# A mixture-of-experts layer on one core: packed expert numbers, a longer loop, and redrawn head, lists and last stores

## What is computed

```python
def cond(x, w, W_base, b_base, As, Bs):              # w: 64 x 8, one row for each sequence of 64 tokens
    out = einsum('btc,oc->bto', x, W_base) + b_base
    h = einsum('btc,erc->bter', x, As)
    return out + einsum('bter,eor,be->bto', h, Bs, w) * 2.0
def ffn(x1):
    scores = softmax(x1 @ gate_w.T)                   # 8 scores for each token
    topk_w, topk_i = top_k(scores, 2)
    topk_w = topk_w / (topk_w.sum(-1) + 1e-20) * 2.5
    y = sum over the two: topk_w * ((silu(x1 @ w_gate[e]) * (x1 @ w_up[e])) @ w_down[e])
    return y + (silu(x1 @ sw_gate) * (x1 @ sw_up)) @ sw_down
return x + ffn(cond(x, cond_8, ...))
```

## Time and profile before

| | |
|---|---|
| median of three runs | 510.59 us (508.84, 510.59, 510.64) |
| the profiled execution | 506.99 us, its span 505.3 us |
| TensorE, matmuls | busy 490.5 us, 97% |
| TensorE, weight loads | busy 448.2 us, 89% |
| VectorE | busy 355.4 us, 70% |
| ScalarE | busy 261.1 us, 52% |
| GpSimd | busy 249.9 us, 49% |
| instruction fetches | q8: 17 of 0.28 MB in all; q14: 21 of 0.17 MB |
| granted TensorE clock, mean | 0.999 |

### The profile page before, as it was taken

The page is one execution under the profiler, slowest core; times in us unless marked ns, Lnnn a source line. Parts: engine busy times, 40 slices in busy tenths (PEclk is TensorE's granted clock), DMA queues, the critical chain, the costliest instruction groups (busy, mean ns, idle before and its releaser), DMA issues.

```text
span 505.3 us, 10018 instructions
## 1 busy us (share of the span) xinstructions
PE 490.5 (97%) x3071; PEld 448.2 (89%) x3072; DVE 355.4 (70%) x765; ACT 261.1 (52%) x525; POOL 249.9 (49%) x367
## 2 busy tenths in 40 slices
PE   8999999999999999989999999999999899999996
PEld 7998988888888889988889999999998899888886
DVE  3666778898987556766676677676675666479896
ACT  3567785556663445565455555545554444444322
POOL 2042246655551454666967767677667674211100
PEclk9999999999999999999999999999999999999999
DMA  8387569156222234534344444444444442599942
GB/s 225 130 281 224 169 186 310 57 179 201 45 83 43 84 93 126 119 103 125 104 114 116 114 116 123 123 117 117 112 114 116 115 105 68 145 370 322 384 140 83
DMA packets 104938, 74.54 MB, mean 148 GB/s; under 512 B 61946, under 2 KB 99844, under 8 KB 104900
## 3 DMA queue, kind: packets, MB, share of 16 engines
q1 hardware_dynamic: 95780, 55.21, 37.1%
q0 software_dynamic: 6816, 18.62, 12.5%
q10 hardware_dynamic: 2304, 0.26, 0.5%
HBM read 40.25 MB, written 20.32 MB: 120 GB/s over the span
## 4 chain that ended last, share of the span: by engine, by line
PE 75%; DVE 15%; ACT 5%; issue 4%; DMA 1%; another core or an unknown queue 0%; DVEq 0%; ACTq 0%
PE bank L274 17%; PE bank L276 17%; PE bank L275 17%; PE bank L790 9%; PE bank L762 5%; PE bank L792 5%; DVE bank L1222 2%; ACT gt_h L952 1%; DVE acc L1333 1%; DVE xt_l L1034 1%; ACT x_half L872 1%; DVE x L1058 1%; DVE pos L1081 1%; DMA xin<-in_x_dram 1%; PE bank L576 1%
## 5 line engine op out<-in xcount | busy, mean ns | idle before, releaser
L274 PE MATMUL bank<-w_all,rt_h 128*128 x284 | 97.6, 344 | 0.0
L276 PE MATMUL bank<-w_all,rt_l 128*128 x284 | 91.6, 323 | 0.0
L275 PE MATMUL bank<-w_all,rt_h 128*128 x284 | 91.5, 322 | 0.0
L790 PE MATMUL bank<-w_all,gt_h 128*128 (+1 forms) x213 | 78.0, 396 | 0.2 <-issue 0.2
L551 POOL DMA_INDIRECT y_rows<-y_sb,dst_i x71 | 72.5, 1021 | 11.2 <-POOL spare L465 10.4
L544 POOL DMA_INDIRECT rows<-x_halves,tok_i x71 | 69.5, 978 | 12.5 <-issue 2.2
L952 ACT CAST gt_h<-bank 128x512 fp32r<-128x512 f32 (+1 forms) x48 | 28.1, 586 | 88.7 <-DVE bank L1222 79.8
L274 PE MATMUL bank<-xs_h,sg_h 128*128 128x512 f32 x176 | 70.6, 401 | 0.3 <-DVE gt_h L1233 0.3
L275 PE MATMUL bank<-xs_l,sg_h 128*128 128x512 f32 x176 | 68.9, 391 | 0.0
L276 PE MATMUL bank<-xs_h,sg_l 128*128 128x512 f32 x176 | 68.7, 390 | 0.0
L1295 DVE TENSOR_TENSOR g<-bank,act 128x352 f32<-128x352 f32 x71 | 37.2, 524 | 41.7 <-issue 24.5
(11 more groups left out here) (180 smaller groups left out, 1155.6 us busy)
## 6 DMA issues: line engine op xcount, KB each, us to landing
pick<-y_rows SPq DMA_DIRECT2D x16, 512.0 KB, 7.8
xin<-in_x_dram SPq DMA_DIRECT2D x8, 512.0 KB, 4.8
x_halves<-x_half SPq DMA_DIRECT2D x8, 512.0 KB, 3.3
w_own<-in_L_ffn_w_gate_dram SPq DMA_DIRECT2D x8, 352.0 KB, 4.5
w_own<-in_L_ffn_w_up_dram SPq DMA_DIRECT2D x8, 352.0 KB, 4.7
y_sb<-in_x_dram SPq DMA_DIRECT2D x5, 512.0 KB, 3.5
base_rows<-y_sb SPq DMA_DIRECT2D x5, 512.0 KB, 2.8
acc<-base_rows SPq DMA_DIRECT2D x5, 512.0 KB, 7.1
```

Of the source, the lines that this page charges most:

```text
L274: pe.matmul(o, lh, rh, start=start, stop=False, skip_group_check=skip)
L275: pe.matmul(o, lh, rl, start=False, stop=False, skip_group_check=skip)
L276: return pe.matmul(o, ll, rh, start=False, stop=stop, skip_group_check=skip)
L790: pe.matmul(YE[par][:, 0:2 * D].rearrange("p (h d) -> p h d", h=2), gt_h[par][0:n, cols], both, start=(c == 0), stop=False, skip_group_che ...
```

## The change

- *Head.* On SP: W_base first, then x in two loads of 256 rows with a semaphore each (`s_x_two`, `s_xin[0]`), then cond, then bias. g_raw and b_row go to ACT's queue, ahead of lora_b. TensorE turns W_base, g_raw and b_row before x, x in halves, with the folds between. ScalarE and VectorE take the halves of W_base (`base_high`, `base_low`) around those of x.
- *Ranks and one-hots.* `rank` moves from behind unit 5 to behind the gate of unit 6. In each fifth unit two tiles of one-hots for three, so tile 31 is made in unit 23 and the lists in unit 24. In unit 8 two of cost for three ahead of the low half, so the compare L1168 stands behind it.
- *Expert numbers.* blk_e stays in fp32; seven multiply-adds fold eight numbers into one word, base 8 (`words`), in units 26 and 27. TensorE loads a word for eight blocks and takes a number out with a shift and a mask (`expert_in`).
- *Loop.* Block 0, eight blocks written out, three turns of 16 blocks, 14 blocks written out.
- *Before block 0.* ScalarE: silu of block 0 ahead of the rounding of rows 1. VectorE: product of block 0 ahead of the low half of rows 1.
- *End.* The last low half in two instructions of 256 columns, TensorE waits for the second only from the third tile on; the store of the middle piece is issued by ACT.

```diff
-    TURN = 12
+    TURN, PER = 16, 8
-            first.append(min(first[-1] + (1, 3, 3, 3, 3, 1)[w % NC], NT))
+            first.append(min(first[-1] + (1, 3, 3, 3, 2, 1)[w % NC], NT))
...
-            load_x(0)
             sp.dma_start(base_raw[:], ...).then_inc(s_dw, 16)
-            sp.dma_start(g_raw[:], gate_w).then_inc(s_dg, 16)
-            sp.dma_start(b_row[:], ...).then_inc(s_dc, 16)
+            for first, here in ((0, s_x_two), (2, s_xin[0])):
+                sp.dma_start(xin[0][:, first:first + 2, :],
+                             x_rows[first * P:(first + 2) * P, :].rearrange("(t p) d -> p t d", p=P)).then_inc(here, 16)
+            sp.dma_start(cond_in[:], cond).then_inc(s_dcond, 16)
...
             gate(j, c)
+                if u == RANK_AT + 1:
+                    rank()
...
-                if u == RANK_AT:
-                    rank()
...
+            def e_steps(first, count, w):
+                words = {0: word_at(w)}
+                def number(n):
+                    if n // PER not in words:
+                        words[n // PER] = word_at(w + n // PER)
+                    return expert_in(words[n // PER], n % PER)
+                before, expert = number(0), number(1)
+                for s in range(count):
+                    before, expert = expert, e_step(first + s, (1 + s) % 2, before, expert,
+                                                    (lambda: number(s + 2)) if s + 1 < count else None)
+                return before
+            e_gate_up(0, 0, expert_in(word_at(0), 0), None)
             down(*order[NPRE - 1])
+            e_steps(1, PER, 0)
+            n_turns = (NBLK - 1 - PER) // TURN
             with pe.Fori(0, n_turns) as q:
+                e_steps(q * TURN + (PER + 1), TURN, q * (TURN // PER) + 1)
+            done = n_turns * TURN + PER
+            before = e_steps(done + 1, NBLK - 1 - done, done // PER)
...
             sc.dma_start(a_raw[:], lora_a.rearrange("e r c -> (e r) c")).then_inc(s_da, 16)
-            sc.dma_start(cond_in[:], cond).then_inc(s_dcond, 16)
+            sc.dma_start(g_raw[:], gate_w).then_inc(s_dg, 16)
+            sc.dma_start(b_row[:], b_base.rearrange("(k p) -> k p", p=P)).then_inc(s_dc, 16)
...
             r_word_high(1)
+            e_silu(0)
             r_high(1)
-            e_silu(0)
...
+            sc.wait_ge(s_fin, 2 * (NG - 1) + 2)
+            sc.dma_start(out_rows[T - 2 * P:T - P, :], acc[NG - 1][:, 2, :]).then_inc(s_out, 16)
...
+            def words():
+                digits = blk_e[:].rearrange("p (w j) -> p w j", j=PER)
+                last = digits[:, :, PER - 1]
+                v.wait_ge(s_blk, 1)
+                for j in reversed(range(PER - 1)):
+                    yield small(v.scalar_tensor_tensor(out=last, in0=last, scalar=float(E), in1=digits[:, :, j],
+                                                       op0=ALU.mult, op1=ALU.add))
+                v.tensor_copy(blk_w[:], last).then_inc(s_words, 1)
...
+                    for h in range(2):
+                        cols = slice(h * 2 * P, (h + 1) * 2 * P)
+                        v.tensor_tensor(gt_h[p][HALF:P, cols], G_B[p][0:HALF, cols], gt_h[p][0:HALF, cols].bitcast(F32),
+                                        ALU.subtract).then_inc(s_gl, 1)
...
-            steps_at = {..., 8: (3, 1000)}
+            steps_at = {..., 8: (2, 1000)}
...
             r_word_low(1)
+            e_mul(0)
             r_low(1)
-            e_mul(0)
```

More of the change, by code:

```diff
@@ L444, in _ @@
             last = NG - 1
-            for n, (first, end) in enumerate(((0, 2), (2, 3), (3, 4))):
+            for n, (first, end) in ((0, (0, 2)), (2, (3, 4))):
                 sp.wait_ge(s_fin, 2 * last + n + 1)
@@ L613, in _ @@
             mm.then_inc(s_aT, 1)
-            turn_x(0)
+            pe.wait_ge(s_dw, 16)
+            for k in range(K):
+                for o in range(K):
+                    pe.transpose(bank[2 + k][:, o * P:(o + 1) * P], base_raw[:, o, k * P:(k + 1) * P], ident[:])
             pe.wait_ge(s_dg, 16)
@@ L619, in _, with turn_two, fold @@
             pe.transpose(bank[6][:, K * E:K * (E + 1)], b_row[:], ident[0:K, 0:K]).then_inc(s_gT, 1)
[L620 to L628 removed]
+            def turn_two(k, first):
+                for t in (first, first + 1):
+                    mm = pe.transpose(TX[k][:, t * P:(t + 1) * P], xin[0][:, t, k * P:(k + 1) * P], ident[:])
+                return mm
+            def fold(k):
                 for o in range(K):
@@ L632, in _ @@
                 mm.then_inc(s_fold, 1)
+            pe.wait_ge(s_x_two, 16)
+            for k in range(K):
+                turn_two(k, 0)
+            pe.wait_ge(s_gate, 1)
+            fold(0)
+            pe.wait_ge(s_xin[0], 16)
+            for k in range(K):
+                turn_two(k, 2).then_inc(s_tx, 1)
+            fold(1)
+            pe.wait_ge(s_cond, 1)
+            pe.wait_ge(s_atl, 1)
+            pe.transpose(bank[7][:, K * P:K * P + NB], cond_er[:], ident[0:NB, 0:NB]).then_inc(s_cT, 1)
             lora_in(0)
-            pe.wait_ge(s_wal, K)
             for t in range(2):
@@ L1265, in r_low @@
                                 ).then_inc(s_rtl, 1)
-            todo, place = routing(), places()
-            steps_at = {0: (0, 8), 1: (3, 6), 2: (3, 6), 3: (3, 6), 4: (3, 1000), 5: (0, 6), 6: (0, 6), 7: (3, 7), 8: (3, 1000)}
+            todo, place, packed = routing(), places(), words()
+            steps_at = {0: (0, 8), 1: (3, 6), 2: (3, 6), 3: (3, 6), 4: (3, 1000), 5: (0, 6), 6: (0, 6), 7: (3, 7), 8: (2, 1000)}
             for u in range(NPRE):
```

79 lines of the change are left out of this document (37 added, 42 removed).

## The result

| | before | after |
|---|---|---|
| median, runs | 509.71 us: 505.89, 508.84, 510.59, 510.64 | 514.17 us: 511.86, 513.77, 514.58, 518.25 |
| the profiled execution, its span | 506.99, 505.3 | 514.58, 512.9 |
| head and projection, up to the first shared matmul | 64.3 | 65.3 |
| shared expert, groups 0 to 4, up to block 0's first matmul | 121.2 | 124.4 |
| from there to block 0's transposes of g | 3.54 | 3.08 |

The change made the kernel slower, where I had forecast 2.2 us faster. (A fourth run of the kernel before, 505.89, has come to its three.) By how much depends on the measure: the medians lie 4.5 us apart (0.9%), the ratio on record is 1.0135, 95% interval 1.0089 to 1.0182, which is 6.9 us of 509.7, and the two profiled executions lie 7.6 apart. Ratios leave out executions in a slower state of the chip, medians do not; between the two I go by the ratio.

What follows compares the result with a forecast made beforehand. TensorE's matmuls were taken to bound the kernel nearly everywhere; head 0.2, rank 0, units 0.9, lists -1.0, swap 0.5, loop 1.1 and tail 0.5 sum to 2.2 us gained, 510.59 to 508.4, range 507 to 510.

Steps and rivals of the forecast that it cites:

- SP and blk_e: SP's wait for blk_e before the last two expert loads: result arrives within 0.5 us of before.
- Rank: Rank matmuls behind unit 6's gate: wait at L723 goes, TensorE waits for unit 4's low half instead; 0, upper bound 0.6.
- Units 8 to 11: Compare moved in unit 8, one one-hot tile less in unit 10: 0.9 us gained, bounds 0.6 and 1.0.
- Lists one unit later: Lists made in unit 24, first gather about 1.0 us late: 1.0 us lost before block 0, bounds 0 and 2.3.
- Swap: Before block 0, VectorE's product goes ahead of block 1's low half: 0.5 us gained, at least 0.
- Head: Start of kernel: W_base turned before x, x split, lora_b later; 0.2 us gained, 0.6 gained to 0.5 lost.
- Loop: Routed stage seams: fewer number loads and returns, 1.1 us gained, bounds 0.5 and 1.6.
- The body's size: Loop code: 42 KB stays where TensorE can jump back; 16 blocks make 56 KB, which no row shows.
- rival C: The 56 KB body does not stay, returns refetch pages: 8 us cost, 516.4 us; chance 0.12.
- Tail: End of kernel: last low half cut in two, middle store on ACT; 0.5 us gained, bounds 0.2 and 0.7.
- A: Routed stage's late blocks shrink with number loads, or returns wait for code: 6.2 us gained, 504.4 us; chance 0.18.
- B: Gains handed back by head, lists and seams: 510.3 us taken, 511.4 at the full -0.8; chance 0.25.

Runs made afterwards that it cites:

- e6: Changed kernel with the compare ahead of the low half again in unit 8, lists still in unit 24: 506.5 us, ratio 1.0130 to the kernel before.
- e4: Changed kernel with SP's store of base 0 and next residual load ahead of the wait for blk_e: 505.06 us, ratio 1.0077 to the kernel before.
- e1: Changed kernel with ranks, one-hot schedule and compare as before: 501.68 us, ratio 1.0023 to the kernel before.
- e14: Kernel before with ranks, one-hots and steps of the change alone: 511.18 us, ratio 1.0057 to the kernel before.
- e7: Changed kernel with three one-hot tiles in each fifth unit again, lists in unit 23: 504.4 us, ratio 1.0081 to the kernel before.
- e13: Kernel before with the new head and the swap before block 0 alone: 508.59 us, ratio 0.9991 to the kernel before.
- e2: Changed kernel with the old loop, a number loaded per block, turns of 12, no words: 504.24 us, ratio 1.0054 to the kernel before.
- e15: Kernel before with the swap and turns of 16 blocks, no words, a load per block: 507.8 us, ratio 0.9992 to the kernel before.
- e11: Kernel before with words and turns of 8 blocks, loop ending at block 64: 516.19 us, ratio 1.0087 to the kernel before.
- e16: Kernel before with the new loop of 16 blocks, its words, and the swap: 510.89 us, ratio 1.0028 to the kernel before.
- e17: Kernel before with the swap, words of two numbers and turns of 12, loop ending at block 62: 517.45 us, ratio 1.0133 to the kernel before.
- e12: Kernel before with the new head alone: 510.86 us, ratio 0.9975 to the kernel before.
- e8: Kernel before with the new loop, words, swap and tail alone: 502.81 us, ratio 1.0035 to the kernel before.
- e10: Kernel before with words and the loop of 16 blocks alone: 515.71 us, ratio 1.0036 to the kernel before.
- e5: The changed kernel as it is, run again in the second group: 505.02 us, ratio 1.0113 to the kernel before.
- e9: The kernel before, unchanged, run for its trace in the third group: 508.56 us in a single run.
- e18: Kernel before with the swap, words of six numbers and turns of 12, loop ending at block 66: 515.47 us, ratio 1.0072 to the kernel before.
- e3: Changed kernel with the head of before: 506.36 us, ratio 1.0098 to the kernel before.

## Why the prediction was wrong

*SP and blk_e: the step that failed.* "SP waits for blk_e before the last two expert loads and gets it within 0.5 us of before." It got it 2.3 later. I moved the compare in VectorE's queue, but counted neither where the operations behind it would then fall against GpSimd nor what stands behind that wait in SP's queue, the base store and the residual load. The trace of before had the rows for it: blk_e's 0.19 us ended at 105.41 beside a GpSimd operation that began at 105.34, and what stands behind the compare was bound to come up to 0.7 later, inside that. Undoing the compare (e6) takes the stop for y_sb from 1.5 to 0.3 and 1.7 us from the stage; leaving blk_e late and moving the two SP instructions ahead of the wait (e4) takes that stop away and 1.4 to 1.6 us; e1 and e14 have the whole units part off and on.

*Rank: 0.* It gave 0.5. Counted from the first shared matmul, the `down` behind the ranks starts at 22.84 for 23.36: the wait of 0.6 at L723 is gone, and the one for unit 4's low half, by which I had set its worth to nothing, is 0.2.

*Units 8 to 11: +0.9.* Not gained; they gave the 0.5 of the ranks back. The changed kernel has four small stops for gt_l, 0.9 in all, where the earlier trace rows had one of 0.4 and one of 0.3 for gt_h; in e14 there are four as well. At the `down` of unit 13, just ahead of the base sums, the changed kernel starts at 52.80 and the kernel before at 52.73, but e6, with the compare in its old place, at 52.14. So it was the compare's move that lost it: VectorE was late in the next units too, and what was moved out of one stood in front of the next.

*Lists one unit later: -1.0.* Right in size: TensorE waited 1.08 where 1.0 was forecast (over 1 us, one of my signs of being wrong), and e7 gets back 1.1. The first gather was later than forecast, 4.2 us for 1.0. Of that, 1.0 is the head's; e6, without the late expert numbers, is 1.35 later than before when counted from the first shared matmul, and the other 1.8 came with SP's chain.

*Swap: +0.5.* Right for its stage: 3.54 became 3.08, and 3.82 became 2.87 in e13, and no kernel with the swap has more than 3.18. But with the old loop block 0 gives part of it back: its excess is 0.74 to 0.80 in e2, e13 and e15 and 0.55 to 0.57 without the swap. No run has the swap alone, and e13's time doesn't show it.

*Head: +0.2, bounds -0.5 to +0.6.* The stop for lora_b is 0.9 for the 0.7 forecast. First lora_out over the eight traces with the new head (leaving out e4, below) is at 15.6 in the mean, over the eight with the old one at 15.1 (leaving out e11, e16 and e17): -0.4, within the bounds. The times of e12 and e13 show no loss. The sign of so small a term stays open.

*Loop: +1.1.* Wrong in sign. The seams did shrink: the first load of a word, in block 0, leaves 0.25 idle, the new loop's entry (block 8) and its returns none over 0.15, and in the traces of the first two groups the blocks at its two returns (24 and 40) have no excess over 0.1. The first word of the changed kernel, against the earlier trace rows:

```profile
193.23 0.19 PEld L279 LDWEIGHTS bank<-w_all,rt_h 128*128 128x128 f32 x1 [0.25 <-issue]
```

At the entry nothing of it was left. Where TensorE no longer stands in front of block 1, it stops a block later: every trace with words has 0.13 to 0.79 of excess in block 1, none without words more than 0.08. VectorE stands there until the store of the last base rows has landed, and TensorE waits for the low half behind that. VectorE, then TensorE, after:

```profile
197.86 0.69 DVE L1375 TENSOR_REDUCE y_sb<-bank 128x256 f32<-128x512 f32 x1 [1.60 <-DMA base_rows<-y_sb]
198.46 0.55 DVE L1366 TENSOR_TENSOR gt_l<-bank,gt_h 128x384 fp32r<-128x384 f32 x1
```
```profile
199.15 0.49 PE L820 MATMUL bank<-w_all,gt_h 128*128 x1 [0.41 <-issue]
```

The kernel before had the same wait (0.87), hidden under its stop at the entry. Blocks 0 and 1 together have 0.95 of excess after and 0.63 before; the swap is in the first number. I had counted what a stop costs, and not what is ready behind it.

Four comparisons put loop and words together at a loss of about 2 us: e8 (1.8, interval 1.1 to 2.5, with the swap's gain and the tail inside), e10 (1.8, 0 to 3.7), e16 against e15 (1.8 by the ratios, 3.1 by the medians), e2 against e5 (0.0059 of 501, 3.0, on two chips). Only e8 is clear of noise by itself. On the quiet chips the loss sits in blocks 57, 61 or 62, and 66, and the first of these goes with the fetch behind the exit. In the sixteen traces in which an engine waits for these rows, they came 3.7 to 4.4 us after SP's issue in the eight with a fetch there, and 3.1 to 3.4 in seven of the eight without; e11, without, had 3.9. That this fetch slows the transfer is argued from these traces, not shown by taking it away, and for blocks 61 and 66 it is weaker still, since e11's block 66 was late without one. On the other chips every kernel with words of eight had a stop of 0.8 to 2.0 in block 3, which none without words had (0.14 at most). But that is one of the stands told of below: in e10 VectorE stands 2.50 in front of the product of g in block 3, and the kernel before has 2.46 in front of the same product in block 8, where e10 has none.

```profile
204.32 0.53 DVE L1325 TENSOR_TENSOR g<-bank,act 128x352 f32<-128x352 f32 x1 [2.50 <-issue]
```
```profile
220.50 0.53 DVE L1295 TENSOR_TENSOR g<-bank,act 128x352 f32<-128x352 f32 x1 [2.46 <-issue]
```

e9 and e14, without words, have neither, the changed kernel and e11 both. So the block 3 stop may be a stand in another place rather than a price of the words. e15 shows that the loss isn't the body's length, within its interval of 0.4%. Whether it is the place of the fetches, the shifts in TensorE's queue, VectorE's packing operations or the place of either code in memory stays open, and so does all of the 3.7 and 6.8 us of e18 and e17.

*The body's size.* Right, and rival C false. Of the changed kernel, 281 to 404 us, with the second return (333), the exit (387) and 37 blocks; the instruction queues have only

```profile
q14 instruction: 8, 0.07, 0.2%
```

q8, which fetched in the earlier trace rows during the first turn, is silent. At the first return it did fetch one piece, from 279.8 to 281.2 where block 24's transposes begin at 280.4, and so did e7; that block has 0.13 and 0.10 of excess, and these two are the only traces of this loop without a fetch behind the exit. The other eight traces of this loop have q8 silent over both returns: 56 KB stay where TensorE can jump back. The rule of the Trainium skill that the prediction weighed ("Runtime: NRT & Kernel Launch", Instruction fetch mechanics) is contradicted here as it was for 42 KB.

*Tail: +0.5.* 71.4 became 71.2, but the end behind the last matmul grew from 3.81 to 3.95: 0.1 in all. Cutting the low half gave its 0.25. The store on ACT gave nothing, though SP issues its two remaining stores in 1.01 where the earlier trace rows had 1.39: e2, which has the new tail and the old loop, has 3.82 behind the last matmul, and the kernels of before's tail and loop have 3.80 or 3.81. The 0.15 on top goes with the words: all thirteen traces that have them have 3.95 to 3.97, e10 with the old tail among them. The cause stays open.

*Rivals.* A (late blocks vanish) is false: they belong to VectorE and ScalarE and come whether numbers are loaded or not. B had the direction, but for other reasons. The sum as measured: units and lists -2.9 (e14), loop, words, swap and tail -1.8 (e8), head about 0, together -4.7. The changed kernel is 4.5 us slower by the medians and 6.9 by the ratio, on e5's chip 4.1 and 5.7; up to 2 us are left without a term. The swap and the lists came out as priced; the two terms that decided, blk_e's wait and the loop, were the ones I had taken as free or as a gain. The first of them is shown down to its cause, the second only in part.

## What to carry to other kernels

When an instruction moves in one queue, write down what each engine's queue holds at its new time, and what is queued behind whoever waits for its result; a wait in a DMA queue delays every load behind it, related or not. Keep waits for small results behind the loads that don't need them (e4's shared stage is 1.4 us shorter than e5's, by two lines moved). Before you price the removal of a stop, look which result is ready behind it: the loop's entry gave its gain to a store's landing one block on. And moving work out of a unit in which an engine is late only moves its lateness.

## Of the hardware, not expected

*Some of VectorE's short operations end with GpSimd's.* blk_e takes 0.19, or 1.10 when it starts inside an operation of GpSimd, and then it ends with that: at 107.71, GpSimd's at 107.66. A cast of 128x64 takes 0.20 (L1207), or 1.21 in the same way (L1209, to 103.00, GpSimd's to 102.94). A third case of the changed kernel,

```profile
95.65 1.70 DVE L1197 TENSOR_SCALAR bbase<-bbase 128x8 f32<-128x8 f32 x1
```
```profile
86.73 10.59 POOL L506 TENSOR_TENSOR w_all<-w_own,w_all 128x704 fp32r<-128x704 f32 x8
```

ends at 97.35 beside 97.32; it began inside one subtraction of GpSimd (to 96.62) and lasted over the next one too. In e3 a copy of 128x256 that takes 0.3 elsewhere stood from 241.97 to 245.15, beside two of GpSimd's that ended at 244.97, and TensorE stopped 1.61 us for what followed. Others keep their length: the low half of the earlier trace rows, 0.69 with an input in PSUM, and a reduction of 128x64 (0.22, at 91.57 of the kernel before) lay inside GpSimd's split of the weights, which ran from 85.68 to 96.28. The Trainium skill ("SBUF — State Buffer", Who interferes with whom) has this: copy, cast and tensor_scalar can take the port pair that GpSimd uses, and whoever comes second is blocked for the other's whole instruction. The trace agrees for the casts and tensor_scalars above, the third of which was held over two instructions; the copy of e3 began while GpSimd issued a gather (241.44 to 242.41), ahead of both subtractions.

*The clock after a stop.* TensorE of the changed kernel stopped 2.3 us for g in front of block 18's transposes. The granted clock was at half (1.2 GHz) for 3.4 us from there, only 12 matmuls ran in it, and block 18 had 1.46 of excess on top of the stop (the window, with the granted clock third from the end):

```profile
258.90:262.30 3.40, 3.11 (x12) 3.10 (x13) 1.93 (x5) 1.24 (x4) 1.96 (x4) 0.50 0.31 81
```

e2 had such a spell behind its stop of 1.8 in the shared stage (126.0 long for it). Not every stop of that length was followed by one: the changed kernel's of 2.8 us in front of block 57 was not, nor e16's of 2.2 in front of block 18.

*Stands that belong to the chip.* GpSimd's 2.06 us before the 60th gather was in all twenty traces. The stands of VectorE and ScalarE came in all twelve traces outside the first two groups, in block 56 in all of them and in block 17 or 18 in eleven; nothing in the traces names their cause. They go with the difference between 501 and 508 to 511 us for the same kernel, more than all that the change does. In four traces (e4, e11, e16, e17) the head was 3 to 5 us later, with the new head as with the old.
